# A cross-attention and mixture-of-experts layer on one core: expert weights and scaled tokens turned by DMA, scaling on three engines, the last output projection in quarters

## The reference

```python
x = x + attention(layernorm(x), ctx)   # 16 heads of 128, 4 groups; output projection wo: 2048 -> 256
xt = layernorm(x).reshape(-1, 256)     # 1024 tokens
scores = sigmoid(xt @ gate.T); _, sel = top_k(scores + expert_bias, 2)
for e in range(8):                     # bf16 products, for the tokens that chose e
    xb = (xt * score_e).astype(bf16)
    out += (silu(xb @ w1[e].T) * (xb @ w3[e].T)) @ w2[e].T
out += (silu(xt @ shared_w1.T) * (xt @ shared_w3.T)) @ shared_w2.T
x = x + out
```

## Time and profile before

| | |
|---|---|
| median of 3 runs | 376.64 us (376.41 to 376.7) |
| profiled execution, its time | 377.97 us |
| its span, first to last instruction | 376.3 us |
| PE, DVE, ACT, POOL busy | 91%, 87%, 72%, 44% |
| mean granted clock of PE | 0.977 |

### The profile page before, as it was taken

How to read it: one execution, slowest core, us unless ns; L and a number is a source line. 1 busy time by engine, 2 the same in 40 slices (tenths; PEclk the granted TensorE clock), 3 DMA queues, 4 the chain that set the end, 5 groups by cost and what they waited for, 6 DMA issues and landing times.

```text
span 376.3 us, 7781 instructions
## 1 busy us (share of the span) xinstructions
PE 343.7 (91%) x2471; PEld 237.3 (63%) x2476; DVE 325.6 (87%) x625; ACT 271.2 (72%) x913; POOL 165.8 (44%) x242
## 2 busy tenths in 40 slices
PE   6697798799999999999999999999999999998994
PEld 5373555376567665866685577567666778674572
DVE  1668999998999899899989998999899897759653
ACT  3557879676986797699759876986797567167562
POOL 3356565652754275427344443644174300334330
PEclk9788989999999999999999999999999999989999
DMA  5967000000030003000000000000000000000011
GB/s 179 379 212 223 17 0 2 1 2 14 3 111 0 14 0 111 14 1 0 0 14 0 0 0 14 0 0 0 0 0 1 2 0 2 2 0 3 22 35 57
DMA packets 11603, 13.49 MB, mean 36 GB/s; under 512 B 824, under 2 KB 9024, under 8 KB 11584
## 3 DMA queue, kind: packets, MB, share of 16 engines
q1 hardware_dynamic: 11584, 13.25, 11.0%
HBM read 12.20 MB, written 1.05 MB: 35 GB/s over the span
## 4 chain that ended last, share of the span: by engine, by line
PE 40%; DVE 24%; ACT 17%; issue 10%; POOL 4%; DMA 2%; SPq 1%; DVEq 1%; ACTq 0%; POOLq 0%
PE proj L1324 10%; ACT probs L524 8%; PE pt_ps L1300 5%; DVE probs L953 5%; PE proj L1157 4%; PE turn L1246 3%; DVE nmax L941 3%; DVE pT_lo L879 3%; PE o_ps L1310 3%; POOL q_rot L744 3%; PE sc_ps L1267 2%; ACT pT_hi L435 2%; DMA wq<-in_L_xattn_wq_dram 2%; ACT q_junk L468 2%; DVE q_t L870 2%
## 5 line engine op out<-in xcount | busy, mean ns | idle before, releaser
L524 ACT ACTIVATE probs<-sc_ps,nbias,q_r 128x256 f32<-128x256 f32 x128 | 70.8, 574 | 2.8 <-DVE nbias L945 2.8
L744 POOL TENSOR_TENSOR q_rot<-q_t 128x512 f32<-128x512 f32 x32 | 41.4, 1295 | 42.8 <-DVE q_t L872 42.0
L953 DVE TENSOR_SCALAR probs<-probs,rden 128x256 f32<-128x256 f32 x128 | 51.2, 461 | 1.1
L1157 PE MATMUL proj<-wq_hi,xT 128*128 128x512 f16 x128 | 40.1, 396 | 2.9 <-DVE wq_lo L863 2.9
L435 ACT ACTIVATE pT_hi<-pt_ps 128x512 f16<-128x512 f32 x64 | 34.8, 597 | 10.9 <-PE pt_ps L1300 10.9
L468 ACT ACTIVATE q_junk<-proj 128x128 bf16<-128x128 f32 x128 | 34.0, 295 | 11.7 <-DVE q_t L872 11.7
L879 DVE SCALAR_TENSOR_TENSOR pT_lo<-pt_ps,pT_hi 128x512 f16<-128x512 f32 x64 | 41.0, 682 | 0.6 <-ACT pT_hi L435 0.6
L941 DVE TENSOR_REDUCE nmax<-sc_ps 128x4 f32<-128x1024 f32 x32 | 38.9, 1214 | 1.5 <-PE sc_ps L1289 1.5
L831 POOL TENSOR_TENSOR wq<-xn_all,weight 128x512 bf16<-128x512 f32 x16 | 17.1, 1074 | 44.1 <-DVE weight L1098 23.4
L1324 PE MATMUL proj<-wo_hi,oT_hi 128*128 128x256 f16 x128 | 34.9, 273 | 0.0
L1324 PE MATMUL proj<-wo_lo,oT_hi 128*128 128x256 f16 x128 | 34.9, 273 | 0.0
(11 more groups left out here) (216 smaller groups left out, 920.7 us busy)
## 6 DMA issues: line engine op xcount, KB each, us to landing
wq<-in_L_xattn_wq_dram SPq DMA_DIRECT2D x4, 512.0 KB, 9.1
w<-in_L_ffn_w_dram SPq DMA_DIRECT2D x2, 1024.0 KB, 10.5
wq<-in_L_xattn_wo_dram SPq DMA_DIRECT2D x1, 2048.0 KB, 8.2
ctx_b<-in_ctx_dram SPq DMA_DIRECT2D x8, 128.0 KB, 2.1
out_dram<-x_all SPq DMA_DIRECT2D x4, 256.0 KB, 2.2
x_all<-in_x_dram SPq DMA_DIRECT2D x1, 896.0 KB, 12.3
wkc<-in_L_xattn_wk_ctx_dram SPq DMA_DIRECT2D x1, 512.0 KB, 4.2
wk<-in_L_xattn_wk_dram SPq DMA_DIRECT2D x1, 512.0 KB, 5.1
```

The costliest lines, as they stand in the source:

```text
L524: last = nc.scalar.activation(probs[:, h, :], sc_ps[:, h, :], ACT.Exp, bias=nbias[:, h:h + 1], scale=q_r[:, g, h:h + 1], accum_out=den[:, ...
L744: nc.gpsimd.tensor_tensor(q_rot[:], q_t1[:], q_t2[:], ALU.add).then_inc(q_added, 1)
L953: last = nc.vector.tensor_scalar(probs[:, h, :], probs[:, h, :], rden[:, h:h + 1], None, ALU.mult)
L1157: last = nc.tensor.matmul(bank[:], xT[:, a, c, :], w[:, c, cols], start=(n == 0), stop=(n == 3 * DC - 1))
```

## The change

- Weights: six `dma_start_transpose` on SP, each of 128 x 1024 bf16 from SBUF to SBUF, replace `turn_experts` and its copies. They are issued in rows 2 to 4, behind the casts; PE waits for all six ahead of the first expert.
- Tokens: for each k SP waits for the three scalers and for `expert_up(k - 6)`, and issues one such DMA from `xb` to `xbT`. There are four `xb` and six `xbT` buffers, in memory that attention no longer needs. `turn_tokens` and `e_copy` go.
- Scaling: POOL keeps two tiles, DVE and ACT take one each. A scaling waits until the DMA of k - 4 has landed. ACT and DVE run five experts ahead (`LEAD`).
- The last `out_proj` is cut into four quarters, each behind the `o_low` of its head group, with the turned probabilities and the last `mix` between them. `logits(0)`, the turns of the shared weights and of `xn2` move forward; `gateT`, `sh2T` and two of the `xn2` copies move from DVE to ACT. Router parts 0 and 1 now stand ahead of `p_low(31)` on DVE.
- `shared_down` opens each bank by its first product; the products of zeros go.
- `logits(1)` now stands behind `expert_up(0)` on PE.

The diff cut to its core, indented by eight columns less (declarations of semaphores, two copies that move from DVE to ACT, `turn_shared`, and removed helpers that are printed above are left out):

```diff
@@ -193,10 +193,13 @@
 silu_e = spare[:, 1024:2048].rearrange("p (a t) -> p a t", a=2)
-xbT = spare[:, 2048:3072].bitcast(BF16).rearrange("p (a c t) -> p a c t", a=2, c=DC)
-xb = spare[:, 3072:4096].bitcast(BF16).rearrange("p (a t d) -> p a t d", a=2, t=TT)
+xb_homes = (spare[:, 3072:3584], spare[:, 3584:4096], k_sum[:], k_rot[:])
+xbT_homes = (spare[:, 2048:2560], spare[:, 2560:3072], k_t1[:], k_t2[:], kc_n[:], q_t1[:])
+xb = [h.bitcast(BF16).rearrange("p (c t d) -> p c t d", c=DC, t=TT) for h in xb_homes]
+xbT = [h.bitcast(BF16).rearrange("p (c t) -> p c t", c=DC) for h in xbT_homes]
+NB, NX = len(xb), len(xbT)
+LEAD = 5
 hid_e = wk32[:].rearrange("p c n -> p (c n)")[:, 0:512].bitcast(BF16).rearrange("p (a t) -> p a t", a=2)
-zeros = sb("zeros", [P, P], BF16)
 proj = [stack.enter_context(nc.psum_tensor(f"proj{i}", [P, 512], F32)) for i in range(2)]
@@ -359,9 +351,20 @@
     return up_pairs[(n + 1) % 2]
-gate_ps = (turn[:, 0:TT * E], o_ps[:, 0:TT * E])
-xn2_banks = (proj[1][:], turn[:], sc_a, sc_a)
+gate_ps = (proj[1][:, 0:TT * E], o_ps[:, 0:TT * E])
+xn2_banks = (proj[1][:], turn[:], sc_a, turn[:])
 half_e = (slice(0, E // 2), slice(E // 2, E))
+wT_landed = 16 * 3 * len(half_e)
+def token_turned(eng, k):
+    eng.wait_ge(d_xbT[k % NX], 16 * (k // NX + 1))
+def tile_of(k, t):
+    n, e = k // E, k % E
+    return (xb[k % NB][:, :, t, :], xn2_all[:, n * TT + t, :].rearrange("p (c d) -> p c d", c=DC),
+            weight[:, n * TT + t, e:e + 1])
 block = stack.enter_context(nc.Block())
@@ -411,16 +414,38 @@
+    def turn_up(dst, src):
+        for half in half_e:
+            sp.dma_start_transpose(dst[:, half].rearrange("p e c n -> p (e c) n"),
+                                   src[:, half].rearrange("p e d -> p (e d)")).then_inc(d_wT, 16)
+    def turn_down():
+        for half in half_e:
+            sp.dma_start_transpose(w2T[:, half].rearrange("p e (c q) -> p (e c) q", c=DC),
+                                   w2_b[:, half].rearrange("p e c n -> p (e c n)")).then_inc(d_wT, 16)
     next_ctx(2)
...
     sp.dma_start(w1_32[:], w3.rearrange("e h d -> h e d")).then_inc(d_w3, 16)
+    turn_up(w1T, w1_b)
     next_ctx(4)
...
                  w2.rearrange("e (c p) h -> p (e c) h", p=P)).then_inc(d_w2, 16)
-    with sp.Fori(5, B) as b:
+    turn_up(w3T, w3_b)
+    next_ctx(5)
+    sp.wait_ge(w2_cast, 4)
+    turn_down()
+    with sp.Fori(6, B) as b:
         next_ctx(b)
+    for k in range(E * NT):
+        for scaled in (e_scaled, e_scaled2, e_scaled3):
+            sp.wait_ge(scaled, k + 1)
+        seen(sp, e_up, k - NX + 1)
+        sp.dma_start_transpose(xbT[k % NX].rearrange("p c (t n) -> p (c t) n", t=TT),
+                               xb[k % NB].rearrange("p c t d -> p (c t d)")).then_inc(d_xbT[k % NX], 16)
     with sp.Fori(0, B // 2) as i:
@@ -614,31 +649,17 @@
         copy(dst.rearrange(blocks), bank).then_inc(signal, 1)
...
     def gate_exp(n):
...
                              scale=-1.0).then_inc(g_exp, 1)
-    o_copy(G * B - 2, G - 2)
-    turned(w1T[:, half_e[0]], proj[0][:].bitcast(BF16), t_w1a, r_w1a)
-    gate_exp(0)
-    p_copy(G * B - 1)
-    turned(sh13T[:], turn[:], t_sh13, r_sh13, "p a c n -> p (a c n)")
-    turned(w3T[:, half_e[0]], proj[0][:].bitcast(BF16), t_w3a, r_w3a)
-    o_copy(G * B - 1, G - 1)
-    turned(w2T[:, half_e[0]], pt_ps[:, 0, :].bitcast(BF16), t_w2a, r_w2a, "p e n -> p (e n)")
...
+    def e_scale(k):
+        act.wait_ge(g_weight, k // E + 1)
+        if k >= NB:
+            token_turned(act, k - NB)
+        dst, src, w = tile_of(k, 0)
+        copy(dst, src, w).then_inc(e_scaled3, 1)
     def e_act(k):
@@ -646,22 +667,26 @@
         nc.scalar.activation(silu_e[:, k % 2, :], up_banks(k)[0], ACT.Silu).then_inc(e_silu, 1)
+    o_copy(G * B - 2, G - 2)
+    gate_exp(0)
+    turned(sh13T[:], turn[:], t_sh13, r_sh13, "p a c n -> p (a c n)")
+    xn_copy(2)
+    p_copy(G * B - 1)
+    o_copy(G * B - 1, G - 1)
+    for k in range(LEAD):
+        e_scale(k)
     xn_copy(3)
-    e_copy(0)
     gate_exp(1)
...
         nc.scalar.activation(silu_s, shared_banks(n)[0], ACT.Silu).then_inc(sh_silu, 1)
-        if n == 0:
-            e_copy(1)
         e_act(E * n)
-        e_copy(E * n + 2)
         for k in range(E * n, E * (n + 1)):
...
                 e_act(k + 1)
-            if k + 3 < E * (n + 1) + (2 if n + 1 < NT else 0):
-                e_copy(k + 3)
+            if k + LEAD < E * NT:
+                e_scale(k + LEAD)
 @block.gpsimd
@@ -826,16 +850,18 @@
         pool.wait_ge(g_weight, n + 1)
-        seen(pool, e_turned, k - 1)
+        if k >= NB:
+            token_turned(pool, k - NB)
         tiles = slice(n * TT + TV, (n + 1) * TT)
-        nc.gpsimd.tensor_tensor(xb[:, k % 2, TV:TT, :], xn2_all[:, tiles, :],
-                                weight[:, tiles, e:e + 1].broadcast_to([P, TT - TV, D]),
+        nc.gpsimd.tensor_tensor(xb[k % NB][:, :, TV:TT, :].rearrange("p c t d -> p t c d"),
+                                xn2_all[:, tiles, :].rearrange("p t (c d) -> p t c d", c=DC),
+                                weight[:, tiles, e:e + 1].unsqueeze(3).broadcast_to([P, TT - TV, DC, P]),
                                 ALU.mult).then_inc(e_scaled2, 1)
-    e_scale(0)
-    e_scale(1)
+    for k in range(3):
+        e_scale(k)
     l2_root(B - 1)
-    for k in range(2, E):
+    for k in range(3, E):
         e_scale(k)
@@ -1100,14 +1114,11 @@
     def e_scale(k):
-        seen(dve, e_turned, k - 1)
-        n, e = k // E, k % E
-        dve.wait_ge(g_weight, n + 1)
-        for t in range(TV):
-            last = nc.vector.tensor_scalar(xb[:, k % 2, t, :], xn2_all[:, n * TT + t, :],
-                                           weight[:, n * TT + t, e:e + 1], None, ALU.mult)
-        last.then_inc(e_scaled, 1)
+        dve.wait_ge(g_weight, k // E + 1)
+        if k >= NB:
+            token_turned(dve, k - NB)
+        dst, src, w = tile_of(k, 1)
+        nc.vector.tensor_scalar(dst, src, w, None, ALU.mult).then_inc(e_scaled, 1)
     def e_hidden(k):
@@ -1115,31 +1126,30 @@
                                 ALU.mult).then_inc(e_hid, 1)
-    p_low(G * B - 1)
-    turned(w3T[:, half_e[1]], proj[1][:].bitcast(BF16), t_w3b, r_w3b)
-    xn_copy(2)
-    o_low(G * B - 1, G - 1)
     dve.wait_ge(c_low, 1)
     dve.wait_ge(d_sh, 80)
-    for part in range(4):
-        router(0, part)
-    turned(w2T[:, half_e[1]], sc_a.bitcast(BF16), t_w2b, r_w2b, "p e n -> p (e n)")
+    router(0, 0)
+    router(0, 1)
+    p_low(G * B - 1)
+    router(0, 2)
+    router(0, 3)
+    o_low(G * B - 1, G - 1)
     e_scale(0)
...
     residual(B - 1)
+    e_scale(2)
     second_norm(B - 1)
-    e_scale(2)
+    e_scale(3)
+    e_scale(4)
     for n in range(NT):
...
         nc.vector.tensor_tensor(hid_s, shared_banks(n)[1], silu_s, ALU.mult).then_inc(sh_hid, 1)
-        if n == 0:
-            e_scale(3)
         for k in range(E * n, E * (n + 1)):
...
                 router(1, k)
-            if k + 4 < E * NT:
-                e_scale(k + 4)
+            if k + LEAD < E * NT:
+                e_scale(k + LEAD)
         dve.wait_ge(e_down, E * (n + 1))
@@ -1311,10 +1321,23 @@
         last.then_inc(pv_done, 1)
+    def out_quarter(g):
+        if g == 0:
+            pe.wait_ge(wo_low2, 1)
+            pe.wait_ge(wo_low, 2)
+            pe.wait_ge(r_sh2, 1)
+        pe.wait_ge(o_ready, G * (B - 1) + g + 1)
+        for h in range(g * R, (g + 1) * R):
+            for i, (o, w) in enumerate(((oT_hi, wo_hi), (oT_hi, wo_lo), (oT_lo, wo_hi))):
+                last = nc.tensor.matmul(proj[0][:, 0:D], o[:, g, (h % R) * P:(h % R + 1) * P], w[:, h, :],
+                                        start=(h == 0 and i == 0), stop=(h == H - 1 and i == 2))
+        if g == G - 1:
+            last.then_inc(wo_done, 1)
     def out_proj(b):
         pe.wait_ge(o_ready, G * b + G - 1)
-        if not (isinstance(b, int) and b == B - 1):
-            pe.wait_ge(q_sq, G * b + G + 3)
+        pe.wait_ge(q_sq, G * b + G + 3)
         pe.wait_ge(wo_low2, 1)
@@ -1423,13 +1445,11 @@
                 turn_xn2(0, (q_sq, G * B))
+                turn_xn2(1, (q_ready, G * B))
             if g == 3 and last:
-                turn_xn2(1, (q_ready, G * B))
-                pe.wait_ge(w1_cast, 4)
                 pe.wait_ge(r_sh2, 1)
-                turn_experts(proj[0][:], w1_b, 0, False, t_w1a)
-                pe.wait_ge(n_ready[0], 1)
-                turn_experts(proj[1][:], w1_b, 1, False, t_w1b)
+                logits(0)
+                turn_shared()
             if g:
@@ -1439,46 +1459,23 @@
     U = G * B
-    logits(0)
+    turn_xn2(2, (s_exp, U))
+    out_quarter(0)
     turn_probs(B, 0)
-    pe.wait_ge(g_exp, 1)
-    for a, src in enumerate((sh1, sh3)):
...
-            turned = nc.tensor.transpose(turn[:, (a * DC + c) * P:(a * DC + c + 1) * P],
-                                         src[:, c * P:(c + 1) * P], ident[:])
-    turned.then_inc(t_sh13, 1)
-    pe.wait_ge(w3_cast, 4)
-    pe.wait_ge(r_w1a, 1)
```

(41 more changed lines are left out.)

78 lines of the change are left out of this document (19 added, 59 removed).

## The result

The changed kernel takes 370.52 us, the median of 4 runs (368.07 to 371.11), against 376.52 us (374.57 to 376.7, 4 runs) for the kernel before beside it: a ratio of 0.985 with an interval of 0.981 to 0.988. It is faster, by 6.0 us. I had given 368.5 us with a range of 364 to 387 us, faster at 0.69. Sign and range held; the gain was forecast at 8.1 us. The profiled execution took 370.62 us, with a span of 368.9 us.

The account below looks back on a forecast made before the run. PE was taken to bound the stretch to 323.54 us and the second expert half, DVE the first, a chain through several engines between. Gains 3.2 + 1.2 + 3.3 + 0.15 + 0.3 = 8.1 us gave 368.5 us, range 364 to 387.

Parts of the forecast that it names:

- Weights off PE: Stretch to 323.54 us: 48 weight turns leave PE and four token turns move into a wait; gain 3.2 us.
- Router before `p_low(31)`: DVE before the last projection: two router parts moved ahead cost nothing, with 1 us to spare; no gain credited.
- Shared down product earlier: 323.54 to 336.32 us: first shared down product at 329.8 instead of 334.22 us; further gain 1.2 us.
- Rival (d): PE, with less work and waits for landings, gets the lower clock through the fourteen expert slots: 381 us; chance 0.03.
- The turning DMA: Expert stage: turning DMAs follow each other at pace T = 2.0 us and land in L = 4.0 us.
- rival (a): Expert stage: DMAs are quick, T up to 1.2 us, only PE and DVE bind; span near 365.5 us; chance 0.18.
- Rival (b): Expert stage: DMA queue becomes the bound, span about 328 + 16T us, deciding from T = 3.0 us; chance 0.20.
- (c): Token DMAs far worse, blocks one after the other, 17.6 us a token, above 600 us; chance 0.05.
- (e): Waits on three scalers take what PE frees; within 0.2% of before, 376.6 us; chance 0.03.
- First half of the experts: 336.32 to 350.91 us: one DVE scaling a token instead of two, 11.3 against 14.59 us; gain 3.3 us.
- Between the halves: The 7.85 us between the expert runs: two zero products go, becoming 7.7 us; gain 0.15 us.
- Second half and end: From 358.76 us: five sets of turns leave PE, but the last token lands late, 12.8 us; gain 0.3 us.

Follow-up runs that it names:

- one_piece: Changed kernel with the last projection undone as quarters, all four behind the last mix: 372.4 us, ratio 0.989 to the kernel before.
- weights_router: Kernel before with only the six weight turns by DMA and the router parts in their new places on DVE: 375.1 us, ratio 0.997 to the kernel before.
- warm: Changed kernel with fifty small unused products on PE behind the second gate product: 367.29 us, ratio 0.978 to the kernel before.
- dma_twice: Changed kernel with a second, unused turning DMA of the same size behind each token's: 378.07 us, ratio 1.005 to the kernel before.
- zeros_back: Changed kernel with the products of zeros back in front of both shared down products: 369.46 us, ratio 0.980 to the kernel before.
- after_again: Changed kernel run again without any edit, for scatter: 371.16 us, ratio 0.987 to the kernel before.
- silu_first: Changed kernel with silu's table loaded early on ACT and the first two silu ahead of the second exponential: 365.21 us, ratio 0.972 to the kernel before.
- silu_ahead: silu_first with tokens 5 to 7 and 9 to 15 scaled one or two slots earlier: 366.11 us, ratio 0.974 to the kernel before.

## Why the prediction was right, and where it was not

**Weights off PE (3.2 us forecast, 2.9 measured).** The size came out near, but not for the reason given. "Until 323.54 us PE is busy 14.88 of 15.16 us", and so the 2.65 us of turns are gained, is the step that failed. The weights alone gave 0.1 us. At the start of DVE's product for the shared expert, 25.05 us behind the mark before and 21.81 in the changed kernel, the weights alone bring 0.1 us, the router's new place another 1.2, and the quarters 2.2 (one_piece has it at 24.03); the rest of the new order takes back 0.3. The quarters fill 2.3 us of waits that open on PE once the turns are gone. I wrote that they fill waits, but credited them 0.1 us. No run has the router's place or the quarters with the weights still on PE, so what they would give without the DMAs is not shown.

**Router before `p_low(31)` (nothing forecast).** Right that it costs nothing. That it gives 1.2 us, once the weights are off PE, was missed. "By row durations" DVE's queue from the last low half to the last layer norm could have been added up: router, then four scalings at up to 0.7 us, then `x_all`. I only asked whether the moved parts would delay somebody, not what stood behind them where they were. PE's wait of 0.43 us for `xn_all` at 327.57 us stood in the trace before.

**Shared down product earlier by 1.2 us (0.6 measured).** The stall was named rightly: table load and silu, 3.01 us against 2.8. The rest of the miss is 0.2 to 0.3 us between the shared up product and the last turns, and 0.1 us in the handing over.

**The lower clock (no term in the sum; 1.0 us at once, about 2 in all).** Rival (d) spoke of the clock, but for the whole rest of the kernel and at 0.03. The place in which it came was in my own text: "PE stands for 2.8 us", and the earlier trace rows showed a clock of 0.50 behind a stretch with waits. The kernel before has the lower clock for as long as the changed one, from about 331.6 to 335.0 us against 330.5 to 333.9. But there it falls mostly on the turns of tokens 1 and 2 and the products of zeros, which stood in that gap: it delays the shared down product by about 0.4 us (this starts 1.15 us behind DVE's product, against 0.74 in weights_router at full clock) and makes it 2.26 us instead of 1.97. With the turns gone it falls on the shared down product and the up products behind it, and nothing covers these. This is the missing term. warm shows it at 2.3 us from the mark, of which 1.3 us is certainly clock.

**The turning DMA (T = 2.0, L = 4.0 forecast; 1.3 and 3.3 measured).** Both within the bounds, nearer the lower end. The pace of the queue never set the end; one landing, that of token 7, does stand in the chain that ended last. By my own condition this is nearly rival (a), for which I had 365.5 us. Its 0.7 us for the DMAs in the first half did not come back, since the clock and the landing of tokens 6 and 7 took it. The 1.9 us in the second half came back in part, below. Rival (b) was costed well, as dma_twice shows, and rivals (c) and (e) fell. (By the formula 328 + 16T the estimate of 10.5 us a token makes 496 us, not 490.)

**First half of the experts (3.3 us forecast, 2.9 measured).** 11.73 us against 11.3; with the clock held up and no late landing it is 10.74 us (warm), the 10.6 us of "PE and DVE together". DVE set the slots before, as said. Now it is busy 8.20 us, less than the 9.1 to 10.1 forecast, and PE 10.56. One scaling on ACT took 0.50 us, not 0.4; no run shows that this cost anything. The third scaler is worth 3.5 us in all; the first half has 2.2 us of it (13.92 against 11.73) and the stretches ahead of it 1.4 us.

**Between the halves (0.15 us forecast, −0.06 measured)**: nothing to gain, as zeros_back shows.

**Second half and end (0.3 us forecast, 1.3 measured).** I held the last token against PE at L = 4.0 and T = 2.0; with L = 3.3 and T = 1.3 no expert waits for a DMA there. It is still 11.83 us and not the 10.9 of a full PE: the down products start at 353.54, 355.12, 356.43 and 358.01 us, so that every second slot is 1.58 us instead of 1.31, as PE waits for silu and DVE's product. Even so this step was 1.0 us too careful, which hid most of the clock's cost in the total.

**Sum from the mark:** 2.9 + 0.6 − 1.0 + 2.9 − 0.1 + 1.3 = 6.7 us (the terms rounded), against 8.15 us. That the total came out 2 us off is in part luck: without the second half's 1.0 us the terms would have missed by 2.4 us. From the mark's 6.7 us to the 6.0 us between the medians there remain 0.7 us, no more than the medians of one kernel differ from one set of runs to the next. To set the median 0.3 us above the span was the same as to subtract the gain from the median, and is not at fault: 376.5 − 6.7 = 369.8 us is within 0.8 us of what was measured.

**What stays open.** Tokens 6 and 7 of the changed kernel land in 4.7 us, the others in about 3.3 us. A piece of its chain that ended last, and a window at that time:

```profile
338.71 4.70 DMA wq<-k_rot
```
```profile
339.00:340.00 1.00, 0.69 (x7) 0.50 (x6) 0.93 (x4) 0.73 (x2) 0.04 (x1) 1.00 2.48 69
```

The DMA engines' share is 2.48, so the times of the packets overlap, with only 69 GB/s moved, where 0.93 goes with 181. after_again and zeros_back land the same two tokens in 4.8 and 4.6 us, silu_first token 7 in 5.5 us; warm and silu_ahead have no late landing at these tokens, but warm lands token 4 in 4.4 us. The DMAs for w1 and w3, of the same size, land in 5.4 and 4.8 us, those for w2 in 3.2; they are needed much later. The cause is not known. It costs 0.24 and 0.26 us of PE's waits in the changed kernel and 1.40 us in silu_first.

## What to carry to other kernels

When work is taken out of a full engine, add up the queue of the next engine behind it, from the last shared event to the next; what gives the gain may be the reordering there and not the work removed. When work is taken out of a gap in which PE would otherwise wait, ask for its clock, and on which work the lower clock will then fall, and shorten the gap itself (a table loaded early, silu ahead of an exponential) before covering it. For small gains compare from a common event in the traces, since the part ahead of it scatters by more than the edit is worth.

## What the hardware showed

- A DMA that turns 128 x 1024 bf16 in on-chip memory takes the issuing queue 1.23 to 1.28 us and lands in 3.3 us in most cases (4.4 to 5.6 us in some); in a row they go at a pace of about 1.3 us and take the DMA engines nearly whole (0.93 at 181 GB/s).
- A token's DMA with another of its size behind it (dma_twice) lands in 3.2 to 4.9 us; two landings of 4.7 us in the changed kernel are unexplained.
- Behind a gap of 3.01 us on PE (its work began again at 329.98 us) the granted clock was 0.50 from about 330.5 to 333.9 us; with fifty small products in the gap it stayed at 1.00. It also fell without such a gap, in the kernel before from about 331.6 to 335.0 us, while PE was busy; in weights_router, with the same order of PE's work from the shared product on, it stayed at 1.00. What decides between these two is not shown.
- DVE's scaling of 128 x 256 takes 0.35 us alone; beside POOL's it took 1.13 us in the changed kernel (324.46 us, DVE's timeline), so the stretching known from the earlier trace rows holds for a single one too:

```profile
324.46 1.13 DVE L1121 TENSOR_SCALAR wq<-xn_all,weight 128x256 bf16<-128x256 f32 x1
```
